# Recurrent gate layer and a 64-expert layer in float32 on one core: weight steps split at other points, one gather issued earlier, tensors moved to 128-byte boundaries

## The reference

```
xn = layernorm(x)
q, v = xn @ Wq, xn @ Wv
s[t] = sigmoid(beta) * s[t-1] + v[t]          # scan along the sequence, per feature
y = layernorm(q * s) * ln_g + ln_b
attn = (y * silu(xn @ Wg)) @ Wo
p = softmax(xn @ router_w.T); top 8 of 64 experts, weights normalised to sum 1
xg[e] = the first 128 tokens routed to expert e
ffn = sum over experts of weight * ((silu(xg @ w1) * (xg @ v1)) @ w2)   # hidden size 384
out = x + attn + ffn
```

## Time and profile before

| | us |
|---|---|
| three runs: median (lowest, highest) | 2575.87 (2573.53, 2576.06) |
| the profiled execution's own time | 2576.81 |
| its span, first to last instruction | 2575.1 |
| TensorE matmul busy | 2458.8 (95%) |
| VectorE busy | 1617.9 (63%) |
| ScalarE busy | 1304.7 (51%) |
| GpSimd busy | 673.5 (26%) |
| moved by DMA | 606.46 MB, 236 GB/s on average |

### The profile page before, as it was taken

The page is one execution under the profiler, slowest core; times in us unless marked ns, Lnnn a source line. Parts: engine busy times, 40 slices in busy tenths (PEclk is TensorE's granted clock), DMA queues, the critical chain, the costliest instruction groups (busy, mean ns, idle before and its releaser), DMA issues.

```text
span 2575.1 us, 35371 instructions
## 1 busy us (share of the span) xinstructions
PE 2458.8 (95%) x12113; PEld 2122.8 (82%) x12113; DVE 1617.9 (63%) x1689; ACT 1304.7 (51%) x1435; POOL 673.5 (26%) x523
## 2 busy tenths in 40 slices
PE   7999899899999899999999999999999999999997
PEld 7888678788888788888788888888878888888876
DVE  7676797666665566656566655666556665656653
ACT  5566323554555554555445554445554555544554
POOL 2221122222332232222223222332222221323211
PEclk9899999999999999999999999999999999999998
DMA  7785754896658866679666797666876668866685
GB/s 273 251 309 198 222 187 160 275 299 225 225 192 280 280 208 203 228 243 285 214 229 219 237 286 238 230 208 218 283 235 212 227 221 284 254 229 225 221 249 158
DMA packets 143643, 606.46 MB, mean 236 GB/s; under 512 B 20592, under 2 KB 20656, under 8 KB 143024
## 3 DMA queue, kind: packets, MB, share of 16 engines
q1 hardware_dynamic: 116304, 518.91, 56.8%
q0 software_dynamic: 27232, 86.00, 15.6%
HBM read 520.89 MB, written 100.70 MB: 241 GB/s over the span
## 4 chain that ended last, share of the span: by engine, by line
PE 67%; DVE 11%; DMA 10%; ACT 6%; issue 4%; SPq 1%; POOL 0%; ACTq 0%; DVEq 0%; POOLq 0%
PE psA L1596 14%; PE psA L1597 14%; PE psA L1598 14%; DVE ew_lo L1191 5%; ACT ew_hi L775 5%; DMA pw_raw<-proj_w_dram 5%; PE psH L1596 4%; PE psH L1598 3%; PE psH L1597 3%; DMA ew_raw<-ew_dram 3%; PE psY L1596 3%; PE psY L1598 3%; PE psY L1597 3%; DVE pw_lo L1186 2%; PE psX L1709 2%
## 5 line engine op out<-in xcount | busy, mean ns | idle before, releaser
L1191 DVE TENSOR_TENSOR ew_lo<-ew_raw,ew_hi 128x1536 fp32r<-128x1536 f32 x384 | 694.1, 1817 | 398.1 <-ACT ew_hi L775 386.2
L775 ACT ACTIVATE ew_hi<-ew_raw 128x1536 fp32r<-128x1536 f32 x384 | 567.6, 1483 | 190.8 <-DMA ew_raw<-ew_dram 110.0
L1596 PE MATMUL psA<-xT_hi,pw_hi 128*128 128x512 f32 (+1 forms) x1544 | 615.3, 399 | 20.1 <-issue 16.2
L769 ACT ACTIVATE pw_hi<-pw_raw 128x1024 fp32r<-128x1024 f32 x254 | 267.5, 1060 | 678.4 <-PE psA L1598 606.9
L1597 PE MATMUL psA<-xT_lo,pw_hi 128*128 128x512 f32 (+1 forms) x1544 | 606.9, 393 | 0.0
L1598 PE MATMUL psA<-xT_hi,pw_lo 128*128 128x512 f32 (+1 forms) x1544 | 606.8, 393 | 0.0
L1186 DVE TENSOR_TENSOR pw_lo<-pw_raw,pw_hi 128x1024 fp32r<-128x1024 f32 x256 | 315.3, 1238 | 174.4 <-ACT pw_hi L769 168.5
L1596 PEld LDWEIGHTS psA<-xT_hi,pw_hi 128*128 128x128 f32 x1544 | 294.8, 191 | 80.5 <-issue 23.1
L1596 PE MATMUL psH<-ew_hi,gT_hi 128*128 128x384 f32 x1024 | 345.7, 338 | 6.5 <-DVE ew_lo L1191 6.0
L1598 PEld LDWEIGHTS psA<-xT_hi,pw_lo 128*128 128x128 f32 x1544 | 294.1, 190 | 62.4
L1598 PE MATMUL psH<-ew_hi,gT_lo 128*128 128x384 f32 x1024 | 343.0, 335 | 0.0
(11 more groups left out here) (168 smaller groups left out, 3195.6 us busy)
## 6 DMA issues: line engine op xcount, KB each, us to landing
ew_raw<-ew_dram SPq DMA_DIRECT2D x384, 768.0 KB, 7.5
pw_raw<-proj_w_dram SPq DMA_DIRECT2D x256, 512.0 KB, 4.8
xn_scratch<-xt SPq DMA_DIRECT2D x33, 512.0 KB, 4.6
xt<-x_dram SPq DMA_DIRECT2D x32, 512.0 KB, 5.8
out_dram<-x_dram SPq DMA_DIRECT2D x32, 512.0 KB, 5.6
out_dram<-ot POOLq DMA_DIRECT2D x32, 512.0 KB, 9.4
xn<-xn_turned SPq DMA_DIRECT2D x29, 512.0 KB, 3.6
xn_turned<-xraw SPq DMA_DIRECT2D x28, 512.0 KB, 5.1
```

The lines of the kernel that those rows point to most:

```text
L769: act.activation(dst[:, slot, :, :], pw_raw[:, slot, :, :], ACT.Copy).then_inc(s_pwhi, 1)
L775: act.activation(ew_hi[:, c % 3, :], ew_raw[:, c % 3, :], ACT.Copy).then_inc(s_ewhi, 1)
L1191: dve.tensor_tensor(ew_lo[:, c % 3, :], ew_raw[:, c % 3, :], ew_hi[:, c % 3, :].bitcast(F32), ALU.subtract).then_inc(s_ewlo, 1)
L1596: pe.matmul(dst, l_hi, r_hi_, start=first, stop=False)
```

## The change

Three edits go together.

**Alignment.** Ahead of `xT_hi` the slab pointer is rounded up to a multiple of 128 bytes of the absolute address (32 bytes here). Everything from `xT_hi` on starts on a 128-byte boundary.

```diff
-        slab_bytes = 212576
+        slab_bytes = 212640
@@
         half = place("half", [P, 4], F32)
+        top[0] = -(-(top[0] + slab_at) // 128) * 128 - slab_at
         xT_hi = place("xT_hi", [P, KC, TB], F32R)
```

```diff
 # end of the gate stage, ScalarE
                 proj_hi(None, 0, halfg(j, 8), None, pw2_hi)
+                proj_hi(None, 1, halfg(j, 9), None, pw2_hi)
                 gate(j, 6)
...
                 piece_hi(e + 2, 2)
-                proj_hi(None, 1, halfg(j, 9), None, pw2_hi)
                 gate(j, 7)
                 z_hi_of(j, 6)
+                proj_hi(None, 0, half2(j, 1), ng(j, KC - 2) + 1)
                 piece_hi(e + 2, 3)
-                for w in range(2):
-                    proj_hi(None, w, half2(j, 1), ng(j, KC - 2 + w) + 1)
+                proj_hi(None, 1, half2(j, 1), ng(j, KC - 1) + 1)
 # out stage, ScalarE
             def run_out(j, e, i, last):
+                if i == 2:
+                    for w in range(2):
+                        proj_hi(None, w, half2(j, 3), n2(j, 1, 1) + 1)
                 hT_hi_of(e)
                 if not last:
                     take_xT(j, i)
+                if i == 1:
+                    for w in range(2):
+                        proj_hi(None, w, half2(j, 2), n2(j, 1, 0) + 1, pw2_hi)
                 piece_hi(e + 1, 0)
...
                 piece_hi(e + 1, 2)
-                if i == 1:
+                if i == 3 and not last:
                     for w in range(2):
-                        proj_hi(None, w, half2(j, 2), n2(j, 1, 0) + 1, pw2_hi)
+                        proj_hi(None, w, half2(j, 4), n2(j, 3, 1) + 1)
                 piece_hi(e + 1, 3)
                 out_copy(j, i)
-                if i == 1:
-                    piece_hi(e + 1, 4)
-                    for w in range(2):
-                        proj_hi(None, w, half2(j, 3), n2(j, 1, 1) + 1)
-                    hidden_part(e + 1, c0=5)
...
+                hidden_part(e + 1, c0=4)
 # out stage, SP
+                load_out(4)
                 load_first(e0 + 7, (0,))
-                load_out(4)
                 load_out(5)
                 load_first(e0 + 7, (1, 2))
                 def outp(i, more):
+                    if i == 2 and not last:
+                        load_out(8)
+                        load_out(9)
                     if not last:
                         next_xn(j, i)
-                    load_rest(e0 + 7 + i)
                     if i == 1:
                         load_out(6)
                         load_out(7)
-                        load_first(e0 + 9, range(2))
-                        if not last:
-                            load_out(8)
-                            load_out(9)
-                        load_first(e0 + 9, (2,))
...
+                    load_rest(e0 + 7 + i)
```

```diff
 # TensorE, out_pass
-                        pe.wait_ge(s_go, 16 * j + 8 + 2 * i + 2)
+                        copies = max(i - 1, 0) if isinstance(j, int) and j == 0 else i
+                        pe.wait_ge(s_go, 16 * j + 8 + 2 * copies + 2)
 # TensorE, block 1
                     shift(1, m - 1)
+                if m == KC - 2:
+                    pe.wait_ge(s_mrg, LISTED)
+                    pe.transpose(psX[:, 0, 0:SEL], lf[:, :], ident[0:SEL, 0:SEL]).then_inc(s_lfT, 1)
             shift(1, KC - 1)
-            pe.wait_ge(s_mrg, LISTED)
-            pe.transpose(psX[:, 0, 0:SEL], lf[:, :], ident[0:SEL, 0:SEL]).then_inc(s_lfT, 1)
-            out_pass(1, 0, range(4))
+            out_pass(1, 0, range(3))
             pe.wait_ge(s_ix, 5)
             gather_turn(0)
-            out_pass(1, 1, range(2))
+            out_pass(1, 0, (3,))
             hidden_mm(0)
-            out_pass(1, 1, (2,))
-            hidden_turn(0)
-            output_mm(0)
-            gather_turn(1)
-            out_pass(1, 1, (3,))
-            hidden_mm(1)
```

More of the change, by code:

```diff
@@ L491, in _ @@
                         load_proj(1, NPJ + w + 2)
[L492 to L498, removed]
+                load_first(mm + 1)
             def run(j, e0, last):
@@ L540, in outp @@
                         load_out(7)
-                        load_first(e0 + 9, range(2))
-                        if not last:
-                            load_out(8)
-                            load_out(9)
-                        load_first(e0 + 9, (2,))
[L546 to L551, removed]
+                    load_rest(e0 + 7 + i)
+                    if i == 3 and not last:
+                        load_out(10)
+                        load_out(11)
+                    if more:
+                        load_first(e0 + 8 + i)
                 each_out(last, outp)
@@ L674, in _ @@
                 z_lo_of(1, m)
-            pool.wait_ge(s_x1, 16 * (NTILE - NT))
-            for mm in range(KC // 2):
-                if mm == 0:
+                if m == 4:
                     pool.wait_ge(s_ix, 5)
@@ L683, in _ @@
                     gather(0)
+            pool.wait_ge(s_x1, 16 * (NTILE - NT))
+            for mm in range(KC // 2):
+                if mm == 0:
                     wait_alone(pool, s_acc, 16 * (KC // 2 + 2))
@@ L940, in _, with run_out @@
             z_hi_of(1, KC - 1)
[L941 to L952, removed]
-                    for w in range(2):
[L954 to L968, removed]
+            for c in range(3):
+                piece_hi(0, c, used=False)
+            take_xT(1, 0)
+            gT_hi_of(0)
+            piece_hi(0, 3)
+            out_copy(1, 0)
+            hidden_part(0, c0=4)
+            def run_out(j, e, i, last):
+                if i == 2:
+                    for w in range(2):
+                        proj_hi(None, w, half2(j, 3), n2(j, 1, 1) + 1)
                 hT_hi_of(e)
@@ L1492, in run_out @@
                     xT_lo_of(j, i)
+                if i == 1:
+                    for w in range(2):
+                        proj_lo(n2(j, 2, w), w, (pw2_hi, pw2_lo))
                 piece_lo(e + 1, 0)
@@ L1496, in run_out @@
                 piece_lo(e + 1, 2)
[L1497 removed]
+                if i == 3 and not last:
                     for w in range(2):
[L1499 to L1513 removed]
+                        proj_lo(n2(j, 4, w), w)
+                hidden_part(e + 1)
+            for i in range(1, 4):
+                run_out(1, i - 1, i, False)
             def run(j, e0, last):
@@ L1570, in run @@
                 gate_in(j, 5)
[L1571 removed]
+                for m in (8, 9):
+                    proj_lo(ng(j, m), m % 2, (pw2_hi, pw2_lo))
                 gate_in(j, 6)
@@ L1575, in run @@
                 piece_lo(e + 2, 2)
-                proj_lo(ng(j, 9), 1, (pw2_hi, pw2_lo))
                 gate_in(j, 7)
+                proj_lo(n2(j, 1, 0), 0)
                 piece_lo(e + 2, 3)
-                for w in range(2):
-                    proj_lo(n2(j, 1, w), w)
+                proj_lo(n2(j, 1, 1), 1)
                 lo_z7(j)
@@ L1856, in run_out @@
                 hidden_mm(e + 1)
-            run_out(1, 1, 2, False)
-            run_out(1, 2, 3, False)
+            for i in range(1, 4):
+                run_out(1, i - 1, i, False)
             def run(j, e0, last):
```

116 lines of the change are left out of this document (45 added, 71 removed).

## The result

| kernel | median us | runs | ratio to before, 95% interval |
|---|---|---|---|
| before, same chip | 2574.7 | 4 | 1 |
| changed | 2542.06 (2535.75 to 2549.48) | 4 | 0.9877 [0.9848, 0.9907] |

By the medians the change makes the kernel 32.6 us faster, by the interval 24 to 39 us. A time of 2431 us, 144.6 us less, was forecast; the time lies 2 us above the range of 2405 to 2540 us. The changed kernel's profiled execution took 2535.75 us, with a span of 2534.1.

The account below looks back on a forecast made before the run. TensorE was taken as the bound, busy for 2458.8 of 2575.1 us. 117.6 - 3 + 58 + 11 - 35 - 4 = 144.6 us off 2576.8 gave 2432.2, against the median 2431 us; range 2405 to 2540.

Parts of the forecast that it names:

- Alignment, 117.6 us: Streamed TensorE rows starting on 128-byte boundaries save 11.3 ns in each of 10,408 matmuls, 117.6 us.
- The handover of 2 ns: Part of the 13.3 ns excess, from one matmul to the next, that stays after alignment: 2 ns, read off transposes.
- The first rival: The start address does not matter and only waits go: 2517 us, 2500 to 2555; chance 0.21.
- Hidden at half clock: TensorE's 13.3 ns excess is gone at 1.2 GHz, so something feeds the array at its own pace.
- The split of Wo step 1 moves up: End of the gate stage: splitting step 9 earlier removes 2.6 us and 1.6 us of half clock in 6 blocks, 25 us.
- Wo steps 4 to 7: Out stage: first pair split at step i = 1, successors requested some 9 us earlier; with the gate-end edit 58 us.
- twelve waits: Waits for `hh` in out steps 0 and 2 of blocks 2 to 7, put at 39 us, all removed.
- Blocks 0 and 1, 11 us: Block 0's wait for `ot` goes, net 5 us; block 1's gather runs under gate step 7, 6 us.
- weights late by some 3 us: Block 0: once ScalarE's wait for a tile goes, the weights of Wo step 6 and 7 come late by some 3 us.
- Given back, -35 us: DMA share of 0.93 holds the out stage at 104 us, not 98, giving back 6 us in blocks 1 to 6.
- The slower rival: ScalarE stands still at 12 moved splits for loads in flight, no gain by alignment: 64 us more, 2640 us; chance 0.03.
- The 16.2 us of issue stay: Five TensorE waits named "issue", placed at the loop's end, 16.2 us, remain after the change.

Follow-up runs that it names:

- e1: The kernel before with only its tensors from xT_hi on placed on 128-byte boundaries; 2569.35 us, ratio 1.000.
- the streams: Small kernels that only copy x and stream 48 matmuls of each kind; only profiled: 512 columns took 226.7 ns in float32r on a boundary, 216.0 in bf16.
- e2: The changed kernel with the splits of the last gate steps and of Wo step 1 put back where they were; 2540.69 us, ratio 0.9877.
- e12: The kernel before with SP issuing the loads of the expert's pieces 1 and 2 behind the projection load of m = 9; 2553.77 us, ratio 0.9919.
- e4: The kernel before with only the moved splits and reordered projection loads of blocks 2 to 7; 2552.53 us, ratio 0.9920.
- e9: The changed kernel with SP's projection load ahead of load_rest, block 0's out steps reordered and blocks 2 to 6 written out; 2488.28 us, ratio 0.9666.
- e3: The changed kernel with SP issuing the loads of the expert's pieces 1 and 2 behind the projection load of m = 9; 2523.55 us, ratio 0.9812.

## Why the prediction was wrong

- **Alignment, 117.6 us: the step that failed.** "If the streamed row is fetched in 128-byte lines" turned three widths with one excess into a mechanism, though no row of the trace showed the other case; the prediction said so itself, and still gave it 0.64. Three widths with the same excess say just that the excess doesn't grow with the width. A fixed cost for each float32r matmul says the same: e1, with the rows on boundaries, keeps 227.4 ns and a ratio of 1.000, and the streams show the part in float32r and not in bf16. The term measured 0, within 3 us. The handover of 2 ns, worked out of transposes (0.76 us by 7 is 108.6 ns, not 108.7), was of the right size: the bf16 stream has 2.5 to 2.7 ns. The first rival had it, and its range of 2500 to 2555 us holds the time; its 2517 us were too low because of the next points.
- **Hidden at half clock, "so it is no fixed count of array cycles".** That still holds, but it spoke for no line fetch either. The Trainium skill (TensorE: Matmul & The Clock Gate, "Back-to-back issue gap") gives N / 1.2 ns at 1.2 GHz and N / 2.4 + 2.5 ns at 2.4 GHz, so a part seen only at 2.4 GHz needs no line fetch; our bf16 rows have the 2.5 ns at 2.4 GHz, and no run here has bf16 at 1.2 GHz.
- **"The split of Wo step 1 moves up", 25 us: measured 0, within some 9 us (e2).** The chain named VectorE's low part at 768.90 as what released the load at 770.14. SP's timeline of the kernel before has

```profile
766.02 3.80 SPq L390 DMA_DIRECT2D ew_raw<-ew_dram  x2
770.14 0.34 SPq L514 DMA_DIRECT2D pw_raw<-proj_w_dram  x1
```

so SP was in `load_rest` until 769.82; the low part ended 0.3 us later, and a chain names only the last. The prediction did follow the split past ScalarE's and VectorE's queues, but not past SP's. It also took the load's 9.52 us for a property of the load; most of it was the bytes ahead, 4.2 us being left in e12.
- **"Wo steps 4 to 7", 58 - 25 = 33 us: measured 20.6 with its 95% interval from 16 to 25 (e4).** Mechanism right, size too large: in block 2 TensorE waited 2.56 and 3.38 us for `hh` in steps 0 and 2 before; in e4 it waits 2.54, 0.36, 0.95 and 0.99 us in steps 0 to 3, so a part came back as small waits elsewhere. Over blocks 2 to 7 the waits of step 2 fell from 23.0 to 2.2 us, and those of steps 1 and 3 rose from 2.1 to 5.6, block 7's last one of 3.9 us apart. The prediction's twelve waits come to 37.2 us in the trace, not 39.
- **Blocks 0 and 1, 11 us: 11 us together by the times** (31.6 - 20.6), which is in part luck. Block 1's out stage is 4.9 us shorter, for the 6 forecast; block 0's edit, for which 5 were forecast, is given back in block 1's vq and gate stages. In block 0 the forecast's "weights late by some 3 us" was in truth a tile late by 8.75 us.
- **Given back, -35 us: the change never came near it.** Its stage took 108.30 us, and 104 us at a DMA share of 0.93 were my floor. The floor itself was too high: e9 runs the stage in 101.14 us, TensorE busy for 99.58 of them, at a share of 0.91. Whether DMA would hold back the 98 us that shorter matmuls were to allow, no run shows.
- **The slower rival** asked for loads in flight at the moved splits. ScalarE did stand 2.68 us at 748.99, but e2, which doesn't, is no faster. "The 16.2 us of issue stay" was right (16.6 us), but only four of the five waits, 15.3 us, are at the loop's end; the fifth, of 0.93 us, is at the end of block 0.

## What to carry to other kernels

A pace that is off its ideal by the same amount at each width is first of all a fixed cost for each instruction. Another type in a stream of 48, and another start address in the kernel itself, test it before anything is built on it; the bare stream was no good judge of the address, since it showed differences that the kernel hasn't. Before moving work up so that a load can start sooner, follow the queue that issues the load, and ask what bytes stand ahead of it: here one word in SP's order was worth as much as all the moved splits of blocks 2 to 7 together. And when a chain names a releaser, look whether another ended just before it.

## What the runs showed of the hardware

- float32r at 2.4 GHz: 226.7 ns for 512 columns, 173.8 for 384; bf16 216.0 and 162.5. The difference of 10.7 ns, in 10,408 matmuls of this kernel, would be 111 us or 4.4% of its time. This is an estimate, and a little high, since at half clock nothing of it shows.
- A bare stream's pace of float32r moves between 226.7 and 236 ns with where the operands lie, repeatably, by no rule that these runs found.
- At each of the four jumps back of the long outer loop TensorE stood 3.3 to 4.5 us with no releaser in the trace, and had half clock behind it (a mean clock of 0.59 for the 3.25 us behind block 2 in e3); written out, 34 us were gained, of which 17.8 are the waits of e3's row. The Trainium skill (Advanced Engine Details and Errata, "Control Flow Timing") gives about 51 ns for a branch and about 108 ns for one that compares, an estimate of 0.2 to 0.4 us for the four; the waits here, 16.6 us in the changed kernel, are 40 times that or more. The short inner loops of the vq steps show no such wait. What the time is spent on was not measured.
- The same 512 KB load took 4.1 us issued ahead of 1536 KB (4.2 in e12) and 9.6 us behind 1536 KB issued up to 4 us before it (9.5 in the kernel before).
